# Down projection of a block kernel: each tile's transposes issued after the next tile's matmuls

## What is computed

```python
mod = (silu(c) @ wmod).reshape(8, 6, 1, -1)
sa, ca, ga, sb, cb, gb = (mod[:, i] for i in range(6))
ga = sign(ga) * maximum(abs(ga), 0.25)      # and gb likewise
h = layernorm(x) * (1 + ca) + sa
x = x + ga * local_attn(h, Wq, Wk, Wv, Wo)  # 16 heads of 128, window 512
h = layernorm(x) * (1 + cb) + sb
g = silu((h @ fp8(gate_w)) * gate_scale)    # 2048 -> 6144
u = (h @ fp8(up_w)) * up_scale
x = x + gb * (((g * u) @ fp8(down_w)) * down_scale)   # 6144 -> 2048
```

## Time and profile before

| | us |
|---|---|
| three runs: median (lowest to highest) | 4560.6 (4512.4 to 4853.4) |
| the profiled execution | 4506.6 |
| its span, core 6, the slowest | 4505.1 |
| spans of the eight cores | 4476.3 to 4505.1 |
| TensorE busy with matmuls | 3318.2 (74% of the span) |
| VectorE busy | 806.3 (18%) |
| ScalarE busy | 772.9 (17%) |

### The profile page before, as it was taken

One profiled execution on the slowest core, in us unless ns is written; L12 is line 12 of the kernel. 1 busy time (PEld: TensorE's weight loads), 2 busy tenths in 40 slices (PEclk: granted clock), 3 DMA queues, 4 the chain that ended last, 5 costly groups with the idle time before them and its releaser, 6 DMA issues.

```text
span 4505.1 us, 48731 instructions; the slowest of 8 cores (4476.3 to 4505.1 us)
## 1 busy us (share of the span) xinstructions
PE 3318.2 (74%) x16778; PEld 1542.8 (34%) x16778; DVE 806.3 (18%) x1682; ACT 772.9 (17%) x1329; POOL 406.6 (9%) x536
## 2 busy tenths in 40 slices
PE   3433139996666679699966599976599867599866
PEld 0000014443444444344422244432244323244322
DVE  0001231005555530201100211100211000311000
ACT  0000240125555541210100110000200000200000
POOL 1001000024444440000000000000000000000000
PEclk8555559998888889899988799988799988799988
DMA  6677731379999994212222222312222311222221
GB/s 124 121 126 120 135 84 19 38 66 104 106 105 105 102 114 60 66 66 75 85 86 68 70 75 75 105 64 68 75 77 75 110 65 55 80 79 75 103 68 54
DMA packets 476586, 377.75 MB, mean 84 GB/s; under 512 B 384160, under 2 KB 386912, under 8 KB 469952
## 3 DMA queue, kind: packets, MB, share of 16 engines
q0 software_dynamic: 362688, 148.10, 31.8%
q1 hardware_dynamic: 113664, 226.53, 15.3%
HBM read 505.40 MB, written 62.96 MB: 126 GB/s over the span
## 4 chain that ended last, share of the span: by engine, by line
PE 68%; DMA 14%; issue 7%; DVE 6%; ACT 3%; another core or an unknown queue 1%; DVEq 0%; SPq 0%; ACTq 0%; POOLq 0%; POOL 0%
PE PSf L888 16%; PE PSf L818 14%; PE PSf L828 14%; DMA wmodb<-wmod 6%; PE PSf L498 5%; PE PSf L651 5%; DMA y<-x3p 3%; PE PSf L551 2%; DMA d<-d_scr 2%; PE PSf L534 2%; PE PSf L310 2%; PE PSf L565 2%; DMA s_xe<-x 1%; PE PSf L538 1%
## 5 line engine op out<-in xcount | busy, mean ns | idle before, releaser
L888 PE MATMUL PSf<-fuse,d 128*128 128x512 bf16 x3072 | 707.5, 392 | 239.2 <-DMA d<-d_scr 239.1
L818 PE MATMUL PSf<-h,g 128*128 128x512 bf16 x3072 | 702.5, 382 | 4.5 <-ACT h L790 4.5
L828 PE MATMUL PSf<-h,u8w 128*128 128x512 bf16 x3072 | 694.4, 379 | 0.0
L888 PEld LDWEIGHTS PSf<-fuse,d 128*128 128x128 fp8e4 x3072 | 304.2, 100 | 621.5 <-issue 289.0
L818 PEld LDWEIGHTS PSf<-h,g 128*128 128x128 fp8e4 x3072 | 302.3, 99 | 373.0 <-issue 16.2
L828 PEld LDWEIGHTS PSf<-h,u8w 128*128 128x128 fp8e4 x3072 | 300.5, 98 | 362.5
L845 DVE SCALAR_TENSOR_TENSOR fuse<-PSf,gsus,sy 128x512 bf16<-128x512 f32 x192 | 144.2, 751 | 1253.1 <-ACT sy L840 1253.1
L840 ACT ACTIVATE sy<-PSf,gsus 128x512 bf16<-128x512 f32 x192 | 132.0, 687 | 1164.2 <-PE PSf L828 1164.2
L310 PE MATMUL PSf<-wmodb,csi 128*1 128x512 bf16 x384 | 164.3, 595 | 225.5 <-DMA wmodb<-wmod 211.6
L534 PE MATMUL PSf<-k_fm,q_fm 128*128 128x512 bf16 x256 | 114.4, 447 | 210.6 <-ACT s_p L599 204.3
L574 DVE TENSOR_REDUCE negmax<-PSf 128x1 f32<-128x640 f32 x256 | 209.1, 817 | 222.7 <-PE PSf L540 222.1
(11 more groups left out here) (103 smaller groups left out, 2166.2 us busy)
## 6 DMA issues: line engine op xcount, KB each, us to landing
wmodb<-wmod POOLq DMA_DIRECT2D x64, 768.0 KB, 7.8
g<-g_scr SPq DMA_DIRECT2D x192, 256.0 KB, 2.6
u8w<-u_scr SPq DMA_DIRECT2D x192, 256.0 KB, 2.9
d<-d_scr SPq DMA_DIRECT2D x64, 768.0 KB, 4.9
s_x<-x SPq DMA_DIRECT2D x16, 1024.0 KB, 4.9
s_u<-x SPq DMA_DIRECT2D x16, 1024.0 KB, 5.0
s_xe<-x SPq DMA_DIRECT2D x16, 1024.0 KB, 4.9
y<-x3p SPq DMA_DIRECT2D x64, 256.0 KB, 2.5
```

The lines of the kernel that those rows point to most:

```text
L818: ev("pe", lambda e, par=par, kc=kc: e.matmul(bankf(0 + par), g8[:, par, :].rearrange("p (c n) -> p c n", c=16)[:, kc, :].bitcast(F8), h2[ ...
L828: ev("pe", lambda e, par=par, kc=kc: e.matmul(bankf(2 + par), u8w[:, par, :].rearrange("p (c n) -> p c n", c=16)[:, kc, :].bitcast(F8), h2 ...
L888: ev("pe", lambda e, par=par, m=m, dbk=dbk: e.matmul(bankf(dbk), d8[:, par, :].rearrange("p (a n) -> p a n", a=NM)[:, m, :].bitcast(F8), f ...
```

## The change

The work of a tile is put into two functions, `emit_downmm(dc)` (load, 48 matmuls, VectorE's sum) and `emit_transp(dc)` (the four transposes), and the epilogue of a group into a third, `emit_epilogue(dcg)`. One loop of 17 steps calls them: step `dc` emits load, matmuls and sum of tile `dc`, then the transposes of tile `dc - 1`, and when that was the last of its group, the group's epilogue. The instructions themselves, their operands and their number stay the same, and each wait names the same event as before. The lines are counted anew behind the matmuls: the transposes are line 918, the addition of the epilogue line 931 and the store line 938.

```diff
-        for dcg in range(4):
-            trg0 = c_tr.n
-            for d4 in range(4):
-                dc = dcg * 4 + d4
-                par = dc % 2
...
+        def emit_downmm(dc):
+            par = dc % 2
...
-                    w0 = [(c_fpe, dn_mm_done[dc - 2])]
...
+                w0 = [(c_fpe, dn_mm_done[dc - 2])]
+            ev("sy", lambda e, dc=dc, par=par: e.dma_start(
+                d8[:, par, :], d_scr[dc]),
+               sc=dD8[par], waits=w0)
...
+            brel(dbk, c_fve)
+            stt_y[dc] = c_fve.n
+
+        def emit_transp(dc):
+            par = dc % 2
+            d4 = dc % 4
+            for t4 in range(4):
+                w3 = []
+                if t4 == 0:
+                    w3 = [(c_fve, stt_y[dc])]
+                    if d4 == 0:
+                        w3 += bw(4) + bw(5) + bw(6) + bw(7)
...
+        def emit_epilogue(dcg):
+            TRG = trg_after[dcg]
...
-        dn_prev = dn_mm_done
+
+        for dc in range(NCD + 1):
+            if dc < NCD:
+                emit_downmm(dc)
+            if dc >= 1:
+                emit_transp(dc - 1)
+                if (dc - 1) % 4 == 3:
+                    trg_after[(dc - 1) // 4] = c_tr.n
+                    emit_epilogue((dc - 1) // 4)
+                dn_prev = dn_mm_done
```

More of the change, by code:

```diff
@@ new lines, in build @@
+        stt_y = {}
+        trg_after = {}
+        def emit_downmm(dc):
+            par = dc % 2
+            didx = Q * NCD + dc
+            w0 = []
+            if Q == 0 and dc < 2:
+                w0 = [(c_av, 256), (c_pt, 256), (c_qk, 256),
+                      (dScr2[0], PRE_A), (dScr2[1], PRE_B)]
+            elif dc < 2:
+                w0 = [(c_fpe, dn_prev[14 + dc])]
+            else:
+                w0 = [(c_fpe, dn_mm_done[dc - 2])]
+            ev("sy", lambda e, dc=dc, par=par: e.dma_start(
+                d8[:, par, :], d_scr[dc]),
+               sc=dD8[par], waits=w0)
+            ldd = dD8[par].n
+            dbk = dc % 2
+            for m_ in range(NM):
+                w1 = []
+                if m_ == 0:
+                    w1 = [(dD8[par], ldd), (c_fve, FUSEQ)] + bw(dbk)
+                ev("pe", lambda e, par=par, m=m_, dbk=dbk: e.matmul(
+                    bankf(dbk),
+                    d8[:, par, :].rearrange("p (a n) -> p a n", a=NM)[
+                        :, m, :].bitcast(F8),
+                    fuse[:, m, :], start=(m == 0), stop=(m == NM - 1)),
+                   inc=(c_fpe if m_ == NM - 1 else None), waits=w1)
+            dn_mm_done[dc] = c_fpe.n
+            w2 = [(c_fpe, c_fpe.n)]
+            if Q == 0 and dc == 0:
+                w2 += [(c_mod, 1)]
+            if dc >= 2:
+                w2 += [(c_tr, yev_done[dc - 2])]
+            ev("ve", lambda e, par=par, dc=dc, dbk=dbk, Q=Q:
+               e.scalar_tensor_tensor(
+                   sy2[:, par, :], bankf(dbk), gbds[:, dc:dc + 1],
+                   contrib[:, dc, Q * 512:(Q + 1) * 512],
+                   ALU.mult, ALU.add),
+               inc=c_fve, waits=w2)
+            brel(dbk, c_fve)
+            stt_y[dc] = c_fve.n
@@ new lines, in emit_transp @@
+        def emit_transp(dc):
[7 more added lines that the diff above has]
+                        w3 += bw(4) + bw(5) + bw(6) + bw(7)
+                ev("pe", lambda e, t4=t4, par=par, d4=d4: e.matmul(
+                    bankf(4 + t4)[:, d4 * 128:(d4 + 1) * 128],
+                    sy2[:, par, t4 * 128:(t4 + 1) * 128], id_bf[:, :],
+                    start=True, stop=True),
+                   inc=(c_tr if t4 == 3 else None), waits=w3)
+            yev_done[dc] = c_tr.n
```

## The result

| | before | after |
|---|---|---|
| ten runs of each: median (lowest) | 4511.9 (4492.8) | 4416.0 (4407.9) |
| spans of the eight cores | 4476.3 to 4505.1 | 4380.0 to 4409.8 |
| profiled core, its span | core 6, 4505.1 | core 4, 4409.8 |

The ratio of after to before is 0.9799, with a 95% interval of 0.9784 to 0.9814. In some executions of either kernel the cores of one die or of both ran at a lower granted clock and the time was up to a tenth longer; this ratio, like those further down, compares the others alone. So the change gains 2.0%, with the 2% mark inside the interval. The forecast was 4432 us, or 1.8% less; the measured median is 4416.0.

A forecast was written before the change was run, and what follows sets the result against it. TensorE was taken as busy except for waits on d loads (239.1 us) and VectorE's sum (75.6 us). Hand-overs 72.9 plus stall heads 7.7 made 80.6 us, off the lowest run's 4512.4: 4432 us, range 4400 to 4505.

The forecast's parts named there:

- The hand-overs: Between down tiles without a stall, matmuls no longer wait for VectorE's sum: 18.2 us saved a quarter, 72.9 in four.
- The bound from above: Each transposes-to-matmul hand-over might cost 0.52 us instead of 0.05, taking back 20.7 us at 44 hand-overs.
- The extra 0.45 us: Longer hand-over after tiles that waited for their load; it might stay, 16 × 0.45 = 7.2 us.
- The stalls stay: Three stalls a quarter for the d load remain, moved from before tile 4 to before tile 5 (then 9, 13).
- The head of the stall: From the last matmul's shown end to x3p's start, 1.64 us becomes 1.00: 0.64 less, twelve times, 7.7 us.
- the upper bound: Largest saving allowed, 93 us, with a stall's head gone entirely (12 us more).
- The clock: Slow tiles after stalls, 16 times about 2 us, were left as they are; closing ordinary gaps wins no clock.
- Rival D: Denser down-stage matmuls lower TensorE's clock: over 2% slower, 4763 us with half the tiles at the lower level; chance 0.03.
- B: The stalls in the down stage vanish too, as SyncE's queue keeps its lead: 4218 us; chance 0.03.
- C: TensorE still stops at every down tile, for bank or weights instead of the sum: 4474 us; chance 0.07.

The follow-up runs named there:

- load5_ahead: Kernel before's TensorE order with the changed kernel's SyncE order, one d load ahead of each group's stores; ratio to before 0.9664.
- after_loads_ahead: Changed kernel with every d load issued as soon as its half of the buffer is free, ahead of the epilogue's stores; ratio to before 0.9337.
- before_loads_ahead: Kernel before, its TensorE order kept, with every d load issued as soon as its half of the buffer is free; ratio to before 0.9539.
- lag_in_group: Changed kernel with transposes lagging only inside each group of four, so SyncE's order is that of before; ratio to before 0.9853.
- before_two_sums: Kernel before with VectorE's sum of each tile done twice, a first copy into a spare buffer; ratio to before 1.0136.
- all_loads_ahead: after_loads_ahead with the first two d loads of each quarter also moved ahead of the four s_xe loads; ratio to before 0.9248.

## Why the prediction was right, point by point

**The hand-overs.** Forecast: 18.2 us a quarter. Measured: 23.2 less three stalls' 1.42 each, 18.9, of which 0.7 are a little less of the slow start behind the stalls, so 18.3. In the experiment with the lag inside groups, where 18.9 were expected, the stage is 19.3 us shorter, 0.3 of it in its stalls. The bound from above, 0.52 us for each transposes-to-matmul hand-over, was too high: starts lie 10.58 us apart, and 10.57 was forecast from the gate-to-up pace and the 0.054 us of a further transpose. The extra 0.45 us after tiles 0, 4, 8 and 12 went as well, but the prediction had read it wrongly, as a matter of a tile that had waited for its load. In load5_ahead the tile that waits is tile 5, and the transposes behind it wait only 1.07 us, while those of tile 4, which didn't wait, still wait 1.50. So the extra belongs to the first tile of a group. In the code only its transposes also wait for the four banks of the last epilogue; that this is the cause was not tested. The sum of the forecast isn't touched by it.

**The stalls stay, one tile later.** Shown by the list of waits, 16 pieces before and after, and by SyncE's order. Changing SyncE's order alone removes them (after_loads_ahead, before_loads_ahead).

**The head of the stall** is the term that was mis-sized. It was to be 0.64 us shorter, twelve times, 7.7 us; the stalls became 1.42 us shorter each, 17.0 us. Of this 0.85 is the head (1.72 to 0.87 on the mean). The prediction let x3p start 0.06 us after the shown end of the sum of tile 4. In the trace x3p starts 2329.08 − 2328.41 = 0.67 us after that sum's start, though the sum is shown with 0.75: two instructions of VectorE that don't depend on each other overlap by their ends, which the prediction had allowed TensorE but not VectorE. A part is also that it took the head of before from one stall of 1.64 us, where the mean is 1.72. The other 0.57 us are a shorter chain of stores (8.70 to 8.27) and a shorter load (5.74 to 5.60). No step of the prediction asks for that. It goes with SyncE's order: in the two experiments that keep the stalls and the order of before (lag_in_group, before_two_sums) the means are 8.58 and 8.60 for the chain and 5.78 and 5.77 for the load, and in the changed kernel with two sums 8.37 and 5.58. About half of what the chain lost are single late stores, such as the one of 5.49 us: the medians of before and after are 8.48 and 8.27. Each of these is one execution, and why the order should matter to how fast a store lands is open.

**The sum of the terms.** 4 × 18.3 = 73 us for the hand-overs, where 72.9 were forecast, 17.0 for the stalls and 3 for the slow starts: 93 us, against 80.6. Three quarters of the surplus of 12 us are in the stalls (9.3), and it is what moves the result from 1.8% to 2.0%. The 93 us are the upper bound that the prediction gave, but by another way: there the head of a stall was to go entirely, and it was only halved. That they stay inside the bound is partly luck. The other 4 us between 4432 and 4416 lie in the starting point, 4512.4 us, where the profiled execution took 4506.6.

**The clock.** It was left out of the sum. The slow starts stay, at 1.94 us behind a stall where they were 2.18. That gives the 3 us above, and no step of the change asks for it; in the other kernels with long stalls the mean is 2.02 to 2.14. The dense tiles run at 1.00. By the Trainium skill's rule on the peak-current limiter (TensorE: Matmul & The Clock Gate, Part 1) the denser stage was to be budgeted at 13/16 of the clock; the profiled execution shows nothing of it, with 1.00 on a core whose seven neighbours run the same stage. On all eight cores every tile with no break before it takes the 10.52 us of full pace. Rival D is not what happened.

**Rivals B and C.** B gave the queue a lead that it keeps; it doesn't, but the two kernels with early loads show what the lead is worth, 0.9337 against 0.9799. C wanted another wait at each tile; none is there.

## What to carry to other kernels

Before moving work on one engine, write out what each in-order queue then holds behind it. Here the same new order of loads was worth 3.4% by itself and some 16 us inside the change, by the mean stages of 225.1 us without it and 221.1 with it, because the stores ahead of the next load waited for transposes that the change had put behind 10 us of matmuls. Issue a load where its buffer comes free, not where its tile is computed; that, in one queue and with the same instructions, gave more than the change. And a short dependent step between two long ones (a sum of 0.75 us and its semaphores, 1.4 us a tile) is worth lagging by one stage: it cost little here, where bank and buffer were double already, and it held in every variant tried.

## What the runs showed of the hardware that was not expected

Short breaks of TensorE lost clock in some places and not in others. In load5_ahead, 2330.37 − 2326.21 = 4.16 us lie between the matmuls of tile 4 and tile 5: 1.50 us of waiting, four transposes, and 2.28 us of waiting. Tile 5 took 12.21 us at a granted clock of 0.86. At the start of a quarter in all_loads_ahead, TensorE waits 2.00 to 2.09 us between two matmuls. In 24 of these 32 places on the eight cores, the first two tiles run at full pace, in 8 they take 1.7 us longer. Core 0 has both, in its first quarter and in its last (two rows of its timeline and two of granted clocks):

```profile
2264.67 20.88 PE L886 MATMUL PSf<-fuse,d 128*128 128x512 bf16 x96 [2.09 <-DVE fuse L845]
3973.96 22.57 PE L886 MATMUL PSf<-fuse,d 128*128 128x512 bf16 x96 [2.03 <-DVE fuse L845]
2264.70:2285.40 20.70, 20.70 (x97) 9.36 (x98) 0.75 (x1) 0.00 (x0) 0.00 (x0) 1.00 0.43 153
3974.00:3984.30 10.30, 10.30 (x41) 4.29 (x42) 0.00 (x0) 0.00 (x0) 0.00 (x0) 0.83 0.63 204
```

In the kernel before with two sums, the hand-overs of 2.3 us (2.1 to 3.2 from matmul to matmul) were followed by a slow tile in 53 of 384 cases. In the kernel before, with hand-overs of 1.6 us on the mean, none of the 384 was. So halving a stall, or cutting it to a quarter, gives its own length and little of the roughly 2 us of slow start behind it; removing it gives both. What decides between the two outcomes at the same length of break isn't shown.

A second point is smaller: two VectorE instructions that don't wait for each other, the first shown with 0.75 us, start 0.67 us apart (all 512 pairs of sums in each of the kernels with two sums), so shown durations, summed up, put the end of a row of them too late.
